# A transformer layer on one core: the output norm's statistics, root and scaling, and the first residual, move from inside the gate/up loop to behind it

## The reference

```python
x = L0_attn_x
x = x + _layernorm(_L0_attn_ref(_layernorm(x, axis=-1), ...), axis=-1)
x = x + _layernorm(_L0_ffn_ref(_layernorm(x, axis=-1), w_gate, w_up, w_down), axis=-1)

def _L0_attn_ref(x, ...):                      # its last lines
    attn_out = jnp.einsum('bqhk,hkd->bqd', ctx, Wo) + bo
    y = x + attn_out
    mu = jnp.mean(y, axis=-1, keepdims=True)
    var = jnp.mean(jnp.square(y - mu), axis=-1, keepdims=True)
    return (y - mu) * jax.lax.rsqrt(var + EPS) * gamma + beta

def _L0_ffn_ref(x, w_gate, w_up, w_down):      # 768 hidden, weights are integers / 127
    gate = jnp.einsum('bsd,hd->bsh', x, wg)
    up = jnp.einsum('bsd,hd->bsh', x, wu)
    h = jax.nn.silu(gate) * up
    return jnp.einsum('bsh,dh->bsd', h, wd)
```

## Time and profile before

| | us |
|---|---|
| median of 3 runs (2778.09 to 2781.67) | 2780.82 |
| the profiled execution, its own time | 2779.29 |
| its span, first to last instruction | 2777.5 |
| PE busy in the span | 2679.1 |
| DVE busy | 2349.5 |
| ACT busy | 2437.5 |
| POOL busy | 2275.7 |

### The profile page before, as it was taken

The page is one execution under the profiler, slowest core; times in us unless marked ns, Lnnn a source line. Parts: engine busy times, 40 slices in busy tenths (PEclk is TensorE's granted clock), DMA queues, the critical chain, the costliest instruction groups (busy, mean ns, idle before and its releaser), DMA issues. The chain is left out here.

```text
span 2777.5 us, 83181 instructions
## 1 busy us (share of the span) xinstructions
PE 2679.1 (96%) x34176; PEld 1706.2 (61%) x34176; DVE 2349.5 (85%) x4205; ACT 2437.5 (88%) x4760; POOL 2275.7 (82%) x1919
## 2 busy tenths in 40 slices
PE   6999999999999999999999999999999999889997
PEld 3566666666666666556666666666666666656674
DVE  6888889999989998869888889999999998678775
ACT  5999999999999999889999999999999999856553
POOL 4899999999999998789999999999999999613233
PEclk9999999999999999999999999999999999999998
DMA  4222223111121222132222122221112212221210
GB/s 137 52 60 60 58 55 77 43 35 36 39 43 43 43 43 43 24 91 60 60 58 55 40 49 43 43 43 43 43 43 43 43 41 84 81 77 46 92 54 23
DMA packets 207100, 148.82 MB, mean 54 GB/s; under 512 B 157824, under 2 KB 181632, under 8 KB 206720
## 3 DMA queue, kind: packets, MB, share of 16 engines
q1 hardware_dynamic: 206720, 143.51, 20.8%
HBM read 53.16 MB, written 39.85 MB: 33 GB/s over the span
## 5 line engine op out<-in xcount | busy, mean ns | idle before, releaser
L555 POOL TENSOR_TENSOR p_l<-p_f,p_h 128x512 f16<-128x512 f32 x1536 | 1945.7, 1295 | 84.9 <-ACT p_h L629 81.0
L684 DVE TENSOR_REDUCE mx<-ps_aux 128x1 f32<-128x512 f32 x2048 | 1346.6, 680 | 283.7 <-PE ps_aux L858 270.8
L628 ACT ACTIVATE p_f<-ps_score 128x512 f32<-128x512 f32 x2048 | 1276.9, 626 | 18.8 <-PE ps_score L887 18.6
L629 ACT ACTIVATE p_h<-ps_score 128x512 f16<-128x512 f32 x2048 | 1287.9, 631 | 0.0
L912 PEld LDWEIGHTS ps_ctx<-v_hi_one_lo,p_h 128*128 128x128 f16 x16384 | 880.0, 98 | 245.1 <-POOL p_l L555 1.2
L912 PE MATMUL ps_ctx<-v_hi_one_lo,p_h 128*128 128x65 f16 (+1 forms) x16384 | 908.5, 193 | 1.3 <-POOL p_l L555 1.0
L912 PE MATMUL ps_ctx<-v_hi_one_lo,p_l 128*128 128x65 f16 x8192 | 784.3, 193 | 0.0
L886 PE MATMUL ps_score<-q_hilo,k_hihi 128*128 128x512 f16 x2048 | 776.2, 379 | 4.9 <-ACT p_h L629 3.5
L887 PE MATMUL ps_score<-q_hi_max,k_lo_one 65*128 65x512 f16 x2048 | 778.3, 380 | 0.0
L858 PE MATMUL ps_aux<-k_hihi,q_hilo 128*128 128x512 f16 x2048 | 623.5, 382 | 16.3 <-DVE xTl L763 7.4
L702 DVE TENSOR_TENSOR p_l<-p_f,p_h 128x512 f16<-128x512 f32 x512 | 546.3, 1067 | 18.5 <-ACT p_h L629 18.5
(11 more groups left out here) (188 smaller groups left out, 2156.4 us busy)
## 6 DMA issues: line engine op xcount, KB each, us to landing
v_heads<-v_new SPq DMA_DIRECT2D x64, 288.0 KB, 2.1
v_hi_one_lo<-v_heads SPq DMA_DIRECT2D x32, 576.0 KB, 5.8
heads<-ctx_n SPq DMA_DIRECT2D x128, 128.0 KB, 2.0
x_all<-heads SPq DMA_DIRECT2D x8, 2048.0 KB, 9.2
k_hihi<-hi_st SPq DMA_DIRECT2D x62, 256.0 KB, 4.4
q_hi_max<-hi_st SPq DMA_DIRECT2D x32, 256.0 KB, 3.5
k_lo_one<-lo_st SPq DMA_DIRECT2D x32, 256.0 KB, 4.2
q_hilo<-hi_st SPq DMA_DIRECT2D x31, 256.0 KB, 3.2
```

Of the source, the lines that this page charges most:

```text
L555: nc.gpsimd.tensor_tensor(p_l[:, r], p_f[:, r], p_h[:, r], ALU.subtract).then_inc(lo_pool, 1)
L628: nc.scalar.activation(p_f[:, r], ps_score[:, bank], ACT.Exp, scale=exp_scale)
L629: nc.scalar.activation(p_h[:, r], ps_score[:, bank], ACT.Exp, scale=exp_scale).then_inc(exp_done, 1)
L684: nc.vector.reduce_max(mx[:, blk % 2, tt, ch:ch + 1], ps_aux[:, n % SIDE], AX_X).then_inc(max_read, 1)
```

## The change

Three pieces of turns 1 to 6 are put in another place on DVE, ACT and POOL, the first residual in turns 0 to 6; nothing is added or removed. In turn 7, which has no chain, `moments_o`, `root_o` and `norm_o` stay where they were.

- DVE: `first_residual` stands behind the loop instead of behind block 4; `moments_o` stands between `moments_chain` 2 and `root_chain` 2 instead of behind block 0; `add_x` stands ahead of `residual`.
- POOL: `root_o` stands behind the loop instead of behind block 0.
- ACT: `norm_o` stands behind `norm_residual` instead of ahead of it.

```diff
@@ ACT @@
                 hi_h(FT - 1)
-                if g:
+                if not chains(g):
                     norm_o(g - 1)
                 if chains(g):
                     norm_residual(g + 1)
+                    if g:
+                        norm_o(g - 1)
                     high_normed(g + 1, base(g) + (CT if feeds(g) else 0))
@@ POOL @@
-                    if f == 0 and g:
+                    if f == 0 and not chains(g):
                         root_o(g - 1)
                     if f in (3, 4) and feeds(g):
                         add_half(g + 2, f - 3)
+                if g and chains(g):
+                    root_o(g - 1)
@@ DVE @@
-                    if f == 0 and g:
+                    if f == 0 and not chains(g):
                         moments_o(g - 1)
                     if f == 1 and chains(g):
                         moments_chain(g + 1, 1, z[1 - u])
                     if f == 2 and chains(g):
                         root_chain(g + 1, 1)
-                    if f == 4 and chains(g):
-                        first_residual(g + 1)
                 if chains(g):
+                    first_residual(g + 1)
                     moments_chain(g + 1, 2, x1[(g + 1) % 3])
+                    if g:
+                        moments_o(g - 1)
                     root_chain(g + 1, 2)
+                if feeds(g):
+                    add_x(g + 2)
                 if g:
                     residual(g - 1)
                 if feeds(g):
-                    add_x(g + 2)
                     moments_z(g + 2)
                     root_z(g + 2)
```

## The result

| | before | changed |
|---|---|---|
| median of 4 runs each, on one chip, us | 2779.45 (2777.36 to 2781.67) | 2807.05 (2804.95 to 2807.86) |
| span of the profiled execution, us | 2777.5 | 2805.0 |
| PE / DVE busy, us | 2679.1 / 2349.5 | 2685.9 / 2342.4 |
| length of turns 0 to 6, us | 43.26, 41.14, 41.10 x4, 37.69 | 42.30, 45.54, 47.47, 48.83, 47.57, 43.48, 38.82 |

The ratio is 1.0100 with a 95% interval of 1.0088 to 1.0113. The span grew by 27.5 us and the seven turns, added up, by 27.5 (2771.67 - 2457.66 against 2744.19 - 2457.70, from turn 0's start to turn 7's), so nothing outside them changed.

What follows compares the result with a forecast made beforehand. PE was taken to set the pace. Four late turn starts +29.2, turn 0 -1.1, turn 5 +0.85 and turn 6 +1.5 sum to +30.5 on 2779.29, 2809.8; the median 1.5 above gave 2811, range 2799 to 2819.

Steps and rivals of the forecast that it cites:

- late load, four turns: Starts of turns 2 to 5: PE waits for the heads' data, landing at +46.5 with the next turn otherwise at +41.95.
- lower clock: Starts of turns 2 to 5: PE at half clock after idling 4.9 us, 1.9 us each.
- chain to `xn2`, five turns: Behind the loop, turns 1 to 5: norms and transposes up to the next turn cost 0.85 us more a turn.
- turn 0: No output norm there: its last `lo_c` comes about 1.1 us earlier and nothing fills the gap, -1.1.
- turn 6: PE waits only for the chain to `xn2`: output's statistics add 2.25 us, about 0.75 comes back, +1.5.
- The second residual: Behind the loop: ends at +36.45 instead of +30.00, 6.45 us later, after the output's statistics, root and norm.
- Landing: Heads' load on SP: issued at +36.97, lands at +46.1 to +47.3, with 9.5 us as the middle +46.5.
- Inside the loop: `hf` and `lo_c` come earlier; the last `lo_c` ends at +22.5 instead of +24.0, the projection 1.6 us earlier.
- two blocked root steps: `root_chain` 1 on DVE: POOL's `hTl` of blocks 1 and 2 each block one step by 0.8 to 1.0 us.
- the load in time: Rival: heads' load lands before PE's next turn, leaving the chain alone, +4.7, 2785.5 us; chance 0.05.
- The full clock throughout: Rival at late turn starts: load late but clock stays up, +22.9, 2804 us; chance 0.16.
- The gap: Rival: PE's 2.28 us of waits come back in six turns, -13.7, 2767 us; faster, chance 0.04.

Runs made afterwards that it cites:

- experiment 1: The changed kernel with SP's loads of the heads' data and input issued ahead of the wait for the second residual and its store: 2782.24 us, ratio 1.0014.
- experiment 2: The kernel before with SP's loads issued ahead of the store: 2777.49 us, ratio 1.0001.
- experiment 4: The changed kernel with the first residual put back behind block 4 of the loop: 2808.85 us, ratio 1.0111.
- experiment 8: The changed kernel with only the output's statistics put back behind block 0 of the loop: 2794.39 us, ratio 1.0055.
- experiment 3: The kernel before with only the first residual moved behind the loop: 2774.54 us, ratio 0.9985.
- experiment 7: The kernel before with the first residual behind the loop, POOL's root behind block 1 and SP's loads ahead of the store: 2769.23 us, ratio 0.9966.
- experiment 9: The changed kernel with the output's statistics back behind block 0 and SP's loads ahead of its wait for the second residual: 2770.50 us, ratio 0.9966.

## Why the prediction was right, step by step

Forecast: 2811 us, slower. Measured: 2807.05, in the range. The sum said +30.5 and the turns grew by 27.5. A turn's growth splits with the 41.78 us of experiment 1, in which the load is never late. What a turn of the changed kernel has above that is the wait at its end plus the lower clock at its start. Turn 1: 3.76 above, 3.77 of wait. Turn 2: 5.69, all wait. Turn 3: 7.05, of which 4.51 wait. Turn 4: 5.79, of which 4.07. Turn 5: 1.70, no wait. What is left beside the waits is 2.54, 1.72 and 1.70 us for turns 3, 4 and 5, and half of the time at the lower level, counted above from the clock alone, is 2.6, 1.7 and 1.7.

| term | forecast | measured |
|---|---|---|
| late load, four turns | 4 x (46.5 - 41.95) = 18.2 | 3.77 + 5.69 + 4.51 + 4.07 = 18.04 |
| lower clock | 4 x 1.9 = 7.6 | 0 + 2.54 + 1.72 + 1.70 = 5.96 |
| chain to `xn2`, five turns | 5 x 0.85 = 4.25 | 5 x 0.68 = 3.4 |
| turn 0 | -1.1 | -0.96 |
| turn 6 | +1.5 | +1.13 |
| sum | 30.5 | 27.6 |

- **The second residual:** it ends at +36.41, 6.41 us later than before, for a forecast of +36.45. The serial sum of statistics, root and norm, each by its own row, gave it. Experiments 1 and 2 show that SP's order turns this into the loss, 4 the part of the change that it comes from.
- **Landing:** the loads took 8.5, 10.4, 9.3 and 8.9 us, for 9.5 assumed; the mean is 9.3. Each wait follows its own load. That the sum of the four came within 0.2 us of the forecast is in part luck: the loads landed 0.2 us earlier than assumed on the mean, and the turn without a late load ended 0.17 earlier too.
- **Inside the loop:** `hf` of block 1 at +5.82 (forecast +5.9), of block 3 at +15.54 (+15.5), of block 5 at +20.65 (+20.5, and waiting for `hTl` as told), first residual at +22.57 (+22.5). The two blocked root steps are there, 0.80 and 1.15 us where a free one has 0.16. The step of 1.15 us starts at 2559.55 and ends at 2560.70, while POOL's `hTl` runs from 2559.53 to 2560.68. The Trainium skill, page "SBUF — State Buffer", section "Who interferes with whom", says that a DVE instruction with two SBUF inputs contends with a GpSimd instruction that reads SBUF, over ports that are an exclusive lock; the trace agrees by these times. Without the two blocks I would have forecast 6.8 us less.
- **The chain:** the wait for `xn2` was 1.75 us for a forecast of 2.0, the transposes at +32.82 for +32.85. The projection ended at +31.07, 0.3 later than forecast, so less had been saved ahead of it. The turn came out at 41.78 instead of 41.95 because `low_normed` ended at +41.72 (2585.94 + 1.28) for a forecast of +41.9; PE starts the next turn 0.06 us behind that end in experiment 1.
- **Turn 6:** its wait for `xn2` is 11.97 us where it was 10.25, 1.7 more, and the turn 1.13 longer; the forecast had 2.25 less 0.75.
- **The clock:** the mis-sized term. I let four turn starts fall; three did, and the forecast had no means to tell that turn 2 would keep its clock. The lower clock then cost 2.54, 1.72 and 1.70 us, 1.99 on the mean, close to 1.9. The Trainium skill, page "TensorE: Matmul & The Clock Gate", section "HAM oscillation — how this bites in real kernels", describes a loop in which the work behind every wait for a DMA starts at the lower clock; here the clock fell behind three of four such waits, and behind four of four in experiments 4 and 8.
- **The rivals:** the load in time was excluded by the landings. The full clock throughout would have given 27.6 - 5.96 = 21.6, near its 22.9. The gap did close in part in experiments 3, 7 and 9, but only with the output's statistics inside the loop and the load late by 0.89 us at most.

What is open: why turn 2 kept its clock. I tried nothing on it.

## What to carry to other kernels

Before moving work behind a loop, follow it to the last engine that waits for it, the DMA queue included: a queue runs in order, so a store that waits for a result takes every load behind it along, and a load with 1.5 us of slack appears in no list of waits until that is used up. Issue loads ahead of the store that waits. And judge the pieces of a change one by one, and with the loads out of the way: here all but one of its moves gain 9 us once the loads go first (experiment 9). The same moves lose 15 us with the loads behind the store (experiment 8), and the last one, 2.25 us of statistics, makes that 27.6.

## What was not expected of the hardware

- The length of the idle time did not decide over the clock. Behind 3.77 us of idling PE went on at 1.00 in the changed kernel; behind 3.52 us at the same turn of experiment 8 its first 1.97 us ran at 0.59 on average, and all four starts of experiment 4, behind 4.35 to 5.28 us, at 0.50.
- How much of a turn's start runs at the lower level was not set by the wait either: 2.54 us lost behind 5.69, but 1.72 and 1.70 behind 4.51 and 4.07, and between those two no difference.
- The clock can fall when PE is at work again. Turn 3 began at 0.50, its first matmul took 0.59 us. Turns 4 and 5 began at full clock with matmuls of 0.38 us, and the level fell some 0.7 and 0.9 us later:

```profile
2641.80:2642.40 0.60, 0.60 (x3) 0.29 (x4) 0.00 (x0) 0.00 (x0) 0.00 (x0) 1.00 0.72 236
2642.40:2643.00 0.60, 0.60 (x3) 0.24 (x2) 0.00 (x0) 0.00 (x0) 0.00 (x0) 0.60 0.07 24
...
2689.37:2689.97 0.60, 0.60 (x3) 0.29 (x4) 0.00 (x0) 0.00 (x0) 0.00 (x0) 1.00 0.94 323
2689.97:2690.57 0.60, 0.60 (x4) 0.20 (x2) 0.00 (x0) 0.00 (x0) 0.00 (x0) 0.78 0.05 15
```

- The 2048 KB load took 8.5 to 10.4 us in one kernel, with the same transfers around it each time.
- 64 matmuls whose results nobody reads made the kernel some 8 us shorter, 6.5 of it in turns 1 to 5.
